# Routed expert tiles of a two-layer network: 28 tiles of one expert and four tiles that hold two experts, in place of 36 tiles of one expert

## The chip, the cores and the metric

One NeuronCore of a Trainium2 chip runs the whole program in one launch. The metric is device time in microseconds (us), from the first to the last instruction of the core, taken as the median of several runs of the compiled kernel. All data are fp32. The engines are named as in the profile: PE (TensorE, its matrix multiplications), PEld (its loads of stationary weights), DVE (VectorE), ACT (ScalarE), POOL (GpSimd), SP (SyncE, which here only issues DMAs).

## The reference

Four stages update `x` of 32 rows with 64 tokens of 128 features: attention, a routed expert layer, an autocorrelation stage, and a gated layer with block-wise 4-bit rounding. The change is in the second:

```python
def _L0_ffn_ref(x, Wr, W1, b1, W2, b2):          # x: (32, 64, 128), 8 experts, F_FF = 512, K = 2
    logits = x.mean(axis=1) @ Wr
    top_scores, top_idx = jax.lax.top_k(logits, K)
    weights = jax.nn.softmax(top_scores, axis=-1)
    W1s, b1s = (W1[top_idx], b1[top_idx])
    W2s, b2s = (W2[top_idx], b2[top_idx])
    h = jnp.einsum('btd,bkdf->bktf', x, W1s) + b1s[:, :, None, :]
    h = jax.nn.gelu(h, approximate=False)
    y = jnp.einsum('bktf,bkfd->bktd', h, W2s) + b2s[:, :, None, :]
    return jnp.einsum('bk,bktd->btd', weights, y)
...
x = x + jnp.tanh(g_ffn[0]) * _L0_ffn_ref(_layernorm(x, axis=-1), ...)
```

Each of the 32 rows picks two of eight experts, by its mean over the tokens. So there are 64 pairs of a row and an expert, and each pair is a two-layer network of 128 to 512 to 128 features on 64 tokens.

## The kernel before, in words

The program is written engine by engine, each engine's instructions in a fixed order with semaphores between them. The expert stage works on tiles of two rows (`RPT = 2`, 128 tokens). A tile has one expert, so an expert with an odd number of rows leaves half a tile empty; the program therefore always runs `MOE_TILES = (32 * 2 + 8) / 2 = 36` tiles of 72 slots. Which rows and which expert a tile has is data, computed on the chip; the number of tiles and the order of the instructions are not.

**The routing chain** runs between the second normalisation and the first tile. DVE takes the logits, finds the two best experts and makes one-hot rows (L899 to L907). PE counts rows per expert and the rank of each row (L1365, L1366), DVE turns counts into numbers of tiles (`tcol`, L911, L912), PE sums them over experts (L1369, L1370), DVE compares the sums with the tile numbers (`tend`, L917) and computes each row's slot (`base2`, `slot_t`, `slot_k`, L918 to L922); PE adds up `tend` (L1374) and DVE writes `experts` (L924), the expert of each tile. From one-hot rows of slots (`ohs`, `ohb`, L926, L928), PE packs four row numbers into one code (L1380) and DVE writes `packed` (L932). PE fills the waits of this chain with parts of the next attention stage, which stand between the routing products in its program: `context_tiles` (L1322) and `context_kv` (L1344, with a bias product at L1330).

**The weights.** All experts' weights are loaded to SBUF early (`wall`, 514 KB per expert). SP copies those of one tile into one of six buffers (`feed`, L325 and L328): it reads the expert's number from `experts`, then, from the seventh copy on, waits until the tile that used the buffer has done its second product (`y2_done`), and issues the DMA. Tile `j` uses buffer `j % 6`:

```python
            def feed(j):
                e = sp.value_load(experts[0:1, j:j + 1], min_val=0, max_val=E - 1)
                if j >= 6:
                    sp.wait_ge(m["y2_done"], j - 5)
                sp.dma_start(wbuf[j % 6], wall[:, bass.ds(e, 1), :] ...).then_inc(w_sem[j % 6], 16)
```

**A tile's path.** POOL copies the two rows' tokens into `xg` (`gather`, L413 and L420; between groups of gathers it also works on the 4-bit weights of the last stage, L424 to L437). PE multiplies (`hidden`, L1403): four products of 128x128 weights with 128 tokens. ACT applies Gelu with the expert's bias (`gelu`, L631). PE multiplies again (`second`, L1414): four products accumulated in one bank. DVE adds the result, times the row's weight, to that row of `acc` (`collect`, L960). An fp32 product shows as two records of PE and two of PEld. PE's order is two tiles ahead:

```python
            hidden(0)
            hidden(1)
            for j in range(MOE_TILES):
                if j + 2 < MOE_TILES:
                    hidden(j + 2)
                second(j)
```

A **block** below is one `hidden` or one `second` of one tile: eight records of PE in a row. Other places that the prediction speaks of: `values` (L1159), products on one half of the array's columns (64 of 128, both halves in turn), with `project` before and after it (L1150, L1151); `weigh_values` (L1252), the same with 18 columns of tokens; and POOL's powers for the normalisation (`powers`, L267 to L271) with the small table `codes` behind them (L406).

Of the kernel before, what the change touches and what calls it, by code (L numbers as in the profile page):

```python
# [35 lines left out]
MOE_TILES = (B * TOPK + E * (RPT - 1)) // RPT  # L36
SLOTS = RPT * MOE_TILES
NCOL = max(B, MOE_TILES)
# [9 lines left out]
CODE_MAX = RADIX ** RPC - 1  # L48
CTX_BANK = (4, 6, 7, 4)
# [9 lines left out]
    ("wo0", 2 * D), ("bv_col", 32), ("wo_t", D), ("wr", E), ("iota_e", E), ("iota_s", SLOTS), ("iota_j", MOE_TILES), ("before_b", B), ("ones", P),  # L59
# [43 lines left out]
def build(nc, a):  # L103
    with ExitStack() as ctx:
# [60 lines left out]
        wbuf = [carve(10240 + WEXP * i, WEXP) for i in range(4)] + [carve(25472 + WEXP * i, WEXP) for i in range(2)]  # L165
# [37 lines left out]
        tcol, tend, base2, rank = sm(NCOL), sm(MOE_TILES), sm(E), sm(E)  # L203
        slot_t, slot_k, ohs, ohb, ohw = sm(2, E), sm(2), sm(2, SLOTS), sm(SLOTS), sm(SLOTS)
        codes, packed, experts = sm(RPC), sm(CODES).bitcast(I32), sm(MOE_TILES).bitcast(I32)
# [19 lines left out]
        floors_set hsc_ready xsc_ready rolled_made codes_set xn_d xv_done xm_done xd_done xq_done xqt_done xqt_used gate_done gu_done sg_done hh_done hv_done hm_done hd_done hq_done hq_last ht_done ht_used dn_done x4_done out_done dve_d""".split()  # L225
# [79 lines left out]
        def _(sp):  # L305
# [17 lines left out]
            def feed(j):  # L323

                e = sp.value_load(experts[0:1, j:j + 1], min_val=0, max_val=E - 1)  # L325
# [4 lines left out]
            for j in range(MOE_TILES):  # L330
                feed(j)
# [12 lines left out]
        def _(pool):  # L344
# [6 lines left out]
            pool.memset(acc[:, B:ROWS, :], 0.0).then_inc(m["spare_zero"], 1)  # L351
# [49 lines left out]
            powers(pool, 8, 12)  # L401
            powers(pool, 12, 15)
            powers(pool, 15, 16)
            pool.wait_ge(m["ld_rest"], 16)
            for k in range(RPC):
                pool.tensor_scalar(codes[0:B, k:k + 1], pc("bcol", B), -float(k % RPT), float(RADIX ** k), ALU.add, ALU.mult).then_inc(m["codes_set"], 1)  # L406
# [4 lines left out]
            def gather(first, last):  # L411
                for i in range(first, last):
                    code = pool.value_load(packed[0:1, i:i + 1], min_val=0, max_val=CODE_MAX)  # L413
                    rows = [((code // RADIX ** k) % RADIX).with_bounds(min_val=0, max_val=ROWS - 1) for k in range(RPC)]
# [95 lines left out]
        def _(act):  # L510
# [115 lines left out]
            def gelu(j):  # L626

                act.wait_ge(m["h_done"], j + 1)

                for c in range(FC):  # L630
                    ins = act.activation(hg[j % 3][:, c, :], ps[:, j % 3, RPT * S * c:RPT * S * (c + 1)], ACT.Gelu,  # L631
                                         bias=wbuf[j % 6][:, FF + FC * D + c:FF + FC * D + c + 1])
                ins.then_inc(m["hg_done"], 1)
# [157 lines left out]
        def _(dve):  # L791
# [119 lines left out]
            sr.step(dve.tensor_scalar(tcol[0:E], ps[0:E, 1, 0:NCOL], 1.0 / RPT, (RPT - 1) / (2.0 * RPT), ALU.mult, ALU.add))  # L911
            dve.tensor_scalar(tcol[0:E], tcol[0:E], 1.5 * 2 ** 23, 1.5 * 2 ** 23, ALU.add, ALU.subtract).then_inc(m["route_in"], 1)  # L912
# [4 lines left out]
            dve.tensor_tensor(tend[0:E], ps[0:E, 2, P:P + MOE_TILES], pc("iota_j", E), ALU.is_le).then_inc(m["route_in"], 1)  # L917
            sr.step(dve.scalar_tensor_tensor(base2[0:B], ps[0:B, 0, 0:E], float(RPT), rank[0:B], ALU.mult, ALU.add))  # L918
# [6 lines left out]
            for k in range(2):  # L925
                sr.did(dve.tensor_scalar(ohs[0:B, k, :], pc("iota_s", B), slot_k[0:B, k:k + 1], None, ALU.is_equal))  # L926
# [874 lines left out]
```

## Time and profile before

| | |
|---|---|
| median of 3 runs | 275.0 us (274.87 to 275.17) |
| span of the profiled execution | 274.8 us |
| its busy PE / PEld / DVE / ACT / POOL | 253.9 / 196.4 / 190.7 / 164.6 / 131.0 us |
| expert stage, first to last of its products | 106.9 to 172.5 us of the span |
| mean granted TensorE clock over the span | 0.988 |

The profiled execution has no other time than its span; the runs of the table lie 0.1 to 0.4 us above it. Times in the rows further on are us from the start of the span unless they are marked ns. In groups of instructions, the numbers behind the bar are busy time and the mean ns of one; then the idle time of the engine just before them, with what ended it. The chain is the work that ended last, followed back from the end. The duration of a PE record includes its way through the array, so records overlap and blocks are timed by the distance of their starts.

### The profile page before, as it was taken

The numbers are of one execution on the slowest core, as the hardware profiler recorded it, in microseconds if no ns is written. First come the engines' busy times: TensorE is split into PE (matmuls) and PEld (weight loads), VectorE is DVE, ScalarE is ACT, GpSimd is POOL, SyncE is SP. The second block draws the span as 40 slices with busy tenths as digits, with TensorE's granted clock in tenths as the row PEclk, the third lists the DMA queues.
The fourth block names the chain that finished last, engine by engine and source line by source line (L and its number), as shares of the span: only waits on it lengthen the run. The fifth ranks groups of instructions, "written<-read, shape, count | busy, mean of one in ns | idle before, by whom it ended". The sixth has DMA issues, their size and how long they took to land.

```text
span 274.8 us, 6251 instructions
## 1 busy us (share of the span) xinstructions
PE 253.9 (92%) x2152; PEld 196.4 (71%) x2152; DVE 190.7 (69%) x494; ACT 164.6 (60%) x384; POOL 131.0 (48%) x207
## 2 busy tenths in 40 slices
PE   8999999999899989999999999979998784989886
PEld 6655376666577868999999999665785442766675
DVE  3898688888988763253222223885769989999993
ACT  2369985666488654675566667473445793354453
POOL 4566579999402403218992220275066633353230
PEclk9999999999999998999999999999999999799999
DMA  6999000000000209776777771000000000000111
GB/s 191 379 348 403 13 4 2 2 4 0 2 2 4 76 20 377 300 289 265 296 300 291 292 290 63 2 1 1 4 0 0 0 0 2 0 19 23 38 39 38
DMA packets 12191, 30.11 MB, mean 110 GB/s; under 512 B 1024, under 2 KB 5248, under 8 KB 12032
## 3 DMA queue, kind: packets, MB, share of 16 engines
q1 hardware_dynamic: 12160, 29.71, 28.5%
q8 instruction: 17, 0.28, 0.4%
q14 instruction: 14, 0.11, 0.1%
HBM read 9.71 MB, written 1.05 MB: 39 GB/s over the span
## 4 chain that ended last, share of the span: by engine, by line
PE 64%; DVE 20%; issue 7%; ACT 5%; POOL 2%; DVEq 0%; POOLq 0%
PE ps L1403 12%; PE ps L1414 12%; PE ps L1252 6%; DVE s_region L294 4%; PE ps L1226 4%; PE ps L1239 4%; PE ps L1159 3%; DVE s_region L1090 3%; PE ps L1542 3%; PE ps L1150 2%; DVE s_small L1095 2%; PE ps L1262 2%; PE ps L1151 2%; PE ps L1344 2%; DVE s_small L237 2%
## 5 line engine op out<-in xcount | busy, mean ns | idle before, releaser
L631 ACT ACTIVATE s_region<-ps,s_region 128x128 f32<-128x128 f32 x144 | 40.8, 371 | 21.8 <-PE ps L1403 21.8
L960 DVE SCALAR_TENSOR_TENSOR s_ctxT<-ps,s_region,s_ctxT 128x64 f32 x72 | 18.1, 281 | 43.8 <-PE ps L1414 43.8
L1403 PE MATMUL ps<-s_region 128*128 128x128 f32 x288 | 38.0, 276 | 0.3 <-issue 0.3
L1414 PE MATMUL ps<-s_region 128*128 128x128 f32 x288 | 37.9, 275 | 0.0
L1403 PEld LDWEIGHTS ps<-s_region 128*128 128x128 f32 x288 | 34.9, 192 | 0.7 <-issue 0.7
L1414 PEld LDWEIGHTS ps<-s_region 128*128 128x128 f32 x288 | 35.0, 192 | 0.2 <-issue 0.2
L420 POOL COPY s_region<-s_xt 128x64 f32 x72 | 14.8, 234 | 32.3 <-PE ps L1403 24.5
L574 ACT COPY s_region<-ps 128x512 f32<-128x512 f32 x32 | 17.2, 592 | 16.2 <-PE ps L1239 16.2
L830 DVE TENSOR_REDUCE s_small<-ps 128x16 f32<-128x1024 f32 x16 | 19.6, 1224 | 9.7 <-PE ps L1226 9.7
L1599 PE MATMUL ps<-s_region 128*128 128x352 f32 x64 | 21.1, 469 | 5.3 <-DVE s_region L1090 3.7
L301 POOL TENSOR_TENSOR s_region<-s_region,s_small 128x704 f32<-128x704 f32 (+2 forms) x11 | 14.6, 1330 | 22.0 <-DVE s_region L294 21.7
L364 POOL TENSOR_SCALAR s_region<-s_region 128x512 f32<-128x512 f32 x16 | 24.7, 1569 | 0.0
L267 POOL TENSOR_SCALAR s_small<-s_small 128x4 f32<-128x4 f32 (+3 forms) x14 | 3.2, 232 | 40.8 <-DVE s_small L244 40.8
L294 DVE SCALAR_TENSOR_TENSOR s_region<-s_region 128x704 f32<-128x704 f32 (+2 forms) x28 | 20.4, 728 | 0.5
L1599 PEld LDWEIGHTS ps<-s_region 128*128 128x128 f32 x64 | 11.3, 189 | 11.9 <-DVE s_region L1090 5.2
L838 DVE TENSOR_TENSOR s_region<-ps,s_small 128x1024 f32<-128x1024 f32 x16 | 18.7, 1170 | 0.1
L1252 PE MATMUL ps<-s_region 128*64 128x18 f32 x512 | 17.8, 212 | 0.8 <-ACT s_region L574 0.7
L1252 PEld LDWEIGHTS ps<-s_region 128*64 128x64 f32 x512 | 16.3, 138 | 3.0 <-ACT s_region L574 1.4
L569 ACT ACTIVATE s_region<-s_region 128x1024 f32<-128x1024 f32 x16 | 17.2, 1073 | 1.1 <-DVE s_region L838 1.1
L1226 PE MATMUL ps<-s_region 64*64 64x512 f32 x128 | 17.4, 615 | 0.0
L1239 PE MATMUL ps<-s_par,s_region 128*128 128x128 f32 x128 | 16.7, 273 | 0.0
L269 POOL TENSOR_TENSOR s_small<-s_small,s_par 128x4 f32<-128x4 f32 (+3 forms) x14 | 16.7, 1191 | 0.0
(230 smaller groups left out, 528.7 us busy)
## 6 DMA issues: line engine op xcount, KB each, us to landing
s_region<-s_wall SPq DMA_DIRECT2D x36, 514.0 KB, 3.0
s_wall<-wall SPq DMA_DIRECT2D x8, 514.0 KB, 9.3
s_par<-par SPq DMA_DIRECT2D x1, 1280.0 KB, 10.5
s_x<-x SPq DMA_DIRECT2D x2, 512.0 KB, 6.8
out<-s_x SPq DMA_DIRECT2D x6, 128.0 KB, 1.8
s_region<-ffn SPq DMA_DIRECT2D x1, 560.0 KB, 3.6
s_ctxT<-ctxT SPq DMA_DIRECT2D x2, 256.0 KB, 4.0
s_ctxT<-ctxT SPq DMA_DIRECT2D x1, 512.0 KB, 6.7
```

Source lines behind the costliest of these rows:

```text
L294: return eng.scalar_tensor_tensor(out, mag, 1.5, z, ALU.max, ALU.subtract)
L364: pool.tensor_scalar(kbd[g % 2][:, j, :], cols, hmask[:, j:j + 1], None, ALU.mult).then_inc(m["kbd_done"], 1)
L631: ins = act.activation(hg[j % 3][:, c, :], ps[:, j % 3, RPT * S * c:RPT * S * (c + 1)], ACT.Gelu, bias=wbuf[j % 6][:, FF + FC * D + c:FF + ...
L830: dve.tensor_reduce(mx[t % 2], scores(t % 2), AX, ALU.max).then_inc(m["mx_done"], 1)
L838: dve.tensor_tensor(ssub[t % 2], scores(t % 2), mx[t % 2].unsqueeze(2).broadcast_to([P, H, S]), ALU.subtract).then_inc(m["s_sub"], 1)
L960: dve.scalar_tensor_tensor(row, ps[:, 4 + j % 2, S * k:S * k + S], w, row, ALU.mult, ALU.add).then_inc(m["acc_done"], 1)
L1226: ins = mm(ps[S * row:S * row + S, 2 * (t % 2) + half, :], qT[rows, 2 * t + row, :], kbd[g % 2][rows, :, k:k + S], start=True, stop=True)
L1239: ins = tr(ps[:, 4 + half, P * k:P * k + P], pr[t % 2][:, c:c + P], ident)
L1252: ins = mm(ps[S * row:S * row + S, 6 + t % 2, n * c:n * c + n], pT[t % 2][:, c, S * row:S * row + S], vbd[:, 2 * t + row, c, :], start=Tru ...
L1403: ins = mm(ps[:, j % 3, RPT * S * c:RPT * S * (c + 1)], w[:, P * c:P * c + P], xg[j % 4], start=True, stop=True)
L1414: ins = mm(ps[:, 4 + j % 2, 0:RPT * S], w[:, FF + D * c:FF + D * c + D], hg[j % 3][:, c, :], start=(c == 0), stop=(c == FC - 1))
L1599: ins = mm(ps[:, 1 + 2 * n + t, 0:MLP], xqT[(q // 2) % 2][:, lo:lo + P], wguT[:, MT * P * n:MT * P * n + MLP], start=True, stop=True)
```

## The change

The slots become exactly 64, in 32 tiles. The rows of an expert are paired into whole tiles of one expert; the odd row of an expert goes to a mixed tile, with the odd row of another expert. The program has 28 plain tiles and four mixed ones (tiles 6, 13, 20 and 27; after that four plain ones). If the experts have fewer odd rows, mixed tiles hold two rows of one expert, and the program is the same.

A mixed tile needs two copies of weights, so the copies are numbered apart from the tiles: `FEEDS = 28 + 8 = 36` copies through the same six buffers (`RING`). Copy `f` waits for the tile that read the buffer before, `tile_of(f - 6)`. In a mixed tile each product is made in four parts of 64 weight columns by 64 tokens, one row's tokens with one expert's weights on one half of the array's columns at a time: `pieces` puts both rows on the two halves, and a second turn swaps them. ACT does Gelu in eight parts of 64 tokens, since the bias differs.

The routing chain computes pairs (`qcol`) and odd rows (`ocol`) for each expert, and places of pairs and odd rows. POOL prepares its tables (`routing_tables`: ten instructions, and the four of `codes`, which move with it ahead of two calls of `powers`). The zeroed spare rows of `acc` are no longer needed.

```diff
-MOE_TILES = (B * TOPK + E * (RPT - 1)) // RPT
-SLOTS = RPT * MOE_TILES
+SLOTS = B * TOPK
+MOE_TILES = SLOTS // RPT
+MIXED = E // RPT
+PLAIN = MOE_TILES - MIXED
+RUN = PLAIN // MIXED - 1
+FEEDS = PLAIN + E
+RING = 6
...
+def mixed(j):
+    return j < MIXED * (RUN + 1) and j % (RUN + 1) == RUN
+def first_feed(j):
+    return j + min(j // (RUN + 1), MIXED)
+def tile_of(f):
+    group = RUN + RPT
+    return f - MIXED if f >= MIXED * group else (RUN + 1) * (f // group) + min(f % group, RUN)
...
-                if j >= 6:
-                    sp.wait_ge(m["y2_done"], j - 5)
-                sp.dma_start(wbuf[j % 6], wall[:, bass.ds(e, 1), :].rearrange("p a w -> p (a w)")).then_inc(w_sem[j % 6], 16)
+                if f >= RING:
+                    sp.wait_ge(m["y2_done"], tile_of(f - RING) + 1)
+                sp.dma_start(wbuf[f % RING], wall[:, bass.ds(e, 1), :].rearrange("p a w -> p (a w)")).then_inc(w_sem[f % RING], 16)
...
+            routing_tables()
             powers(pool, 12, 15)
             powers(pool, 15, 16)
...
+                parts, f = (RPT if mixed(j) else 1), first_feed(j)
+                n = RPT * S // parts
+                for k in range(parts):
+                    for c in range(FC):
+                        b1 = wbuf[(f + k) % RING][:, FF + FC * D + c:FF + FC * D + c + 1]
+                        ins = act.activation(hg[j % 3][:, c, n * k:n * k + n], ps[:, j % 3, ...], ACT.Gelu, bias=b1)
...
+            def pieces(j, turn, lo):
+                for half in range(2):
+                    k = half ^ turn
+                    stay = wbuf[(first_feed(j) + k) % RING][:, lo + S * half:lo + S * half + S]
+                    yield slice(S * half, S * half + S), slice(S * k, S * k + S), stay
             def hidden(j):
-                pe.wait_ge(w_sem[j % 6], 16 * (j // 6 + 1))
+                for k in range(RPT if mixed(j) else 1):
+                    pe.wait_ge(w_sem[(f + k) % RING], 16 * ((f + k) // RING + 1))
...
                 for c in range(FC):
+                    if mixed(j):
+                        for turn in range(RPT):
+                            for parts, cols, stay in pieces(j, turn, P * c):
+                                ins = mm(ps[parts, j % 3, RPT * S * c + cols.start:RPT * S * c + cols.stop], stay, xg[j % 4][:, cols], start=True, stop=True)
```

`second` is changed in the same way. What the routing and the expert stage become on the engines is best seen in the order of instructions.

On PE, around tile 6 (`hidden` of tile 5, `second` of 3, `hidden` of 6, `second` of 4, `hidden` of 7). Names behind "waits" are semaphores: `w0` to `w5` count landed weights of a buffer, `xg_done` gathered rows, `hg_done` Gelus, `acc_done` collected rows. Before:

```order
L1403 MATMUL ps<-s_region 128x128 [waits hg_done,xg_done,w5]
L1403 MATMUL ps<-s_region 128x128 x3
L1414 MATMUL ps<-s_region 128x128 [waits acc_done,hg_done]
L1414 MATMUL ps<-s_region 128x128 x3
L1403 MATMUL ps<-s_region 128x128 [waits hg_done,xg_done,w0]
L1403 MATMUL ps<-s_region 128x128 x3
L1414 MATMUL ps<-s_region 128x128 [waits acc_done,hg_done]
L1414 MATMUL ps<-s_region 128x128 x3
L1403 MATMUL ps<-s_region 128x128 [waits hg_done,xg_done,w1]
```

And now, at the same place:

```order
L1470 MATMUL ps<-s_region 128x128 [waits hg_done,xg_done,w5]
L1470 MATMUL ps<-s_region 128x128 x3
L1487 MATMUL ps<-s_region 128x128 [waits acc_done,hg_done]
L1487 MATMUL ps<-s_region 128x128 x3
L1468 MATMUL ps<-s_region 64x64 [waits xg_done,hg_done,w1,w0]
L1468 MATMUL ps<-s_region 64x64 x15
L1487 MATMUL ps<-s_region 128x128 [waits acc_done,hg_done]
L1487 MATMUL ps<-s_region 128x128 x3
L1470 MATMUL ps<-s_region 128x128 [waits hg_done,xg_done,w2]
```

Tile 6 waits for two buffers and has 16 products of 64x64 where four of 128x128 stood, and tile 7 takes the buffer that tile 8 had.

On DVE, in the routing chain, from the counts per expert to the experts of the tiles (`dve_r` is DVE's own count, a wait for its instruction before). Before:

```order
L912 TENSOR_SCALAR s_small<-s_small 8x36 [waits dve_r]
L914 TENSOR_SCALAR s_small<-s_small 32x1 [waits le_ready]
L915 RECIPROCAL s_small<-s_small 32x1 [waits dve_r]
L917 TENSOR_TENSOR s_small<-ps,s_par 8x36 [waits route_mm,dve_r]
L918 SCALAR_TENSOR_TENSOR s_small<-ps,s_small 32x8
L920 TENSOR_TENSOR s_small<-s_small 32x8 [waits dve_r]
L920 TENSOR_TENSOR s_small<-s_small 32x8
L922 TENSOR_REDUCE s_small<-s_small 32x2 [waits dve_r]
L924 TENSOR_SCALAR s_small<-ps 1x36 [waits route_mm,dve_r]
```

And now:

```order
L958 SCALAR_TENSOR_TENSOR s_small<-s_small 8x36 [waits dve_r]
L960 TENSOR_SCALAR s_small<-s_small 32x1 [waits le_ready]
L961 RECIPROCAL s_small<-s_small 32x1 [waits dve_r]
L964 TENSOR_TENSOR s_small<-ps,s_small 8x72 [waits route_mm,dve_r]
L965 TENSOR_TENSOR s_small<-s_small,ps 32x8
L966 TENSOR_TENSOR s_small<-s_small,ps 32x8
L967 TENSOR_TENSOR s_small<-s_small,ps 32x8 [waits dve_r]
L968 TENSOR_TENSOR s_small<-s_small 32x8 [waits dve_r]
L970 TENSOR_TENSOR s_small<-s_small 32x8 [waits dve_r]
L970 TENSOR_TENSOR s_small<-s_small 32x8
L972 TENSOR_REDUCE s_small<-s_small 32x2 [waits dve_r]
L974 TENSOR_SCALAR s_small<-ps 1x36 [waits route_mm,dve_r]
```

One instruction is new ahead of the part shown (L911 and L912 became L956 to L958), and three are new in place of L918, two of them with a wait for the one before.

On PE, the routing products in the same stretch. Before:

```order
L1369 MATMUL ps<-s_small,s_par 8x36 [waits route_in]
L1370 MATMUL ps<-s_par,s_small 32x8
L1322 MATMUL ps<-s_par,s_ctxN 128x128 [waits cf_used,ld_ctxn]
L1374 MATMUL ps<-s_small,s_par 1x36 [waits tr2_used,route_in]
L1322 MATMUL ps<-s_par,s_ctxN 128x128 [waits ld_ctxn]
```

And now:

```order
L1418 MATMUL ps<-s_small,s_par 8x36 [waits tables_set,route_in]
L1419 MATMUL ps<-s_small,s_par 8x36
L1420 MATMUL ps<-s_small,s_par 8x36
L1421 MATMUL ps<-s_small 32x24
L1422 MATMUL ps<-s_par,s_small 32x8
L1370 MATMUL ps<-s_par,s_ctxN 128x128 [waits cf_used,ld_ctxn]
L1426 MATMUL ps<-s_small 1x36 [waits tr2_used,route_in]
L1427 MATMUL ps<-s_small,s_par 1x36
L1370 MATMUL ps<-s_par,s_ctxN 128x128 [waits ld_ctxn]
```

Two products became five, and one became two.

## Rows read from the trace of the kernel before

**Rows 1.** Chain that ended last, expert stage: start us, us, what.
```profile
106.97 2.88 PE ps L1403 x24
...
127.09 1.13 PE ps L1403 x8
...
134.54 1.13 PE ps L1403 x8
135.67 0.89 PE ps L1414 x8
136.56 0.89 PE ps L1403 x8
```
**Rows 2.** Costliest groups of the page: expert stage's ACT, DVE and POOL lines.
```profile
L631 ACT ACTIVATE s_region<-ps,s_region 128x128 f32<-128x128 f32 x144 | 40.8, 371 | 21.8 <-PE ps L1403 21.8
L960 DVE SCALAR_TENSOR_TENSOR s_ctxT<-ps,s_region,s_ctxT 128x64 f32 x72 | 18.1, 281 | 43.8 <-PE ps L1414 43.8
...
L420 POOL COPY s_region<-s_xt 128x64 f32 x72 | 14.8, 234 | 32.3 <-PE ps L1403 24.5
```
**Rows 3.** Chain, earlier stages: half-array blocks and the whole-array products around them.
```profile
7.57 1.90 PE ps L1159 x32
9.47 1.05 PE ps L1150 x2
...
15.20 0.86 PE ps L1150 x2
...
38.97 1.04 PE ps L1252 x32
```
**Rows 4.** Instructions of line L328 (SP's copies of weights): issue to landing.
```profile
DMA to landing us min/median/max: 2.9/3.0/4.9
```
**Rows 5.** DMA view, issues in 101.6:109.3, then one each from 119.7, 134.4, 149.0, 161.6.
```profile
s_region<-s_wall SPq DMA_DIRECT2D x6, 514.0 KB, 2.9
...
s_region<-s_wall SPq DMA_DIRECT2D x1, 514.0 KB, 4.1
...
s_region<-s_wall SPq DMA_DIRECT2D x1, 514.0 KB, 4.9
...
s_region<-s_wall SPq DMA_DIRECT2D x1, 514.0 KB, 4.0
...
s_region<-s_wall SPq DMA_DIRECT2D x1, 514.0 KB, 4.4
```
**Rows 6.** DMA view, queues in 106.9:172.5: packets, MB, share of 16 engines.
```profile
q8 instruction: 4, 0.07, 0.4%
q14 instruction: 5, 0.04, 0.2%
```
**Rows 7.** Page, DMA queues of the whole span: packets, MB, share of 16 engines.
```profile
q8 instruction: 17, 0.28, 0.4%
```
**Rows 8.** Timeline of SP: six first copies, first waited copy; chain: the block ahead.
```profile
101.69 7.56 SPq L328 DMA_DIRECT2D s_region<-s_wall  x6
...
110.86 0.49 SPq L328 DMA_DIRECT2D s_region<-s_wall  x1
...
109.84 0.89 PE ps L1414 x8
```
**Rows 9.** Timeline, 98.85:100.4, routing: start us, us, engine line op out<-in.
```profile
98.96 0.17 DVE L911 TENSOR_SCALAR s_small<-ps 8x36 f32<-8x36 f32 x1
99.17 0.17 DVE L912 TENSOR_SCALAR s_small<-s_small 8x36 f32<-8x36 f32 x1
...
99.39 0.23 PE L1369 MATMUL ps<-s_small,s_par 8*8 8x36 f32 x2
99.46 0.20 PE L1370 MATMUL ps<-s_par,s_small 8*32 8x8 f32 x2
...
99.88 0.14 DVE L918 SCALAR_TENSOR_TENSOR s_small<-ps,s_small 32x8 f32<-32x8 f32 x1
100.06 0.23 DVE L920 TENSOR_TENSOR s_small<-s_small 32x8 f32<-32x8 f32 x2
```
**Rows 10.** Windows: us, PE PEld DVE ACT POOL busy (x), PEclk, DMA share, GB/s.
```profile
98.00:101.00 3.00, 2.33 (x20) 1.55 (x18) 2.31 (x17) 2.60 (x5) 0.00 (x0) 1.00 0.00 0
102.00:105.00 3.00, 3.00 (x8) 1.87 (x8) 0.77 (x5) 1.17 (x2) 1.14 (x6) 0.50 0.72 285
```
**Rows 11.** Timeline of POOL, 88:96: the wait before `powers` and the table `codes`.
```profile
92.88 0.24 POOL L267 TENSOR_SCALAR s_small<-s_small 128x3 f32<-128x3 f32 x1 [3.74 <-DVE s_small L244]
...
95.22 0.85 POOL L406 TENSOR_SCALAR s_small<-s_par 32x1 f32<-32x1 f32 x4
```

More of the change, by code:

```diff
@@ L163, in build @@
         ctxF = carve(8192, TILES * P)
-        wbuf = [carve(10240 + WEXP * i, WEXP) for i in range(4)] + [carve(25472 + WEXP * i, WEXP) for i in range(2)]
+        wbuf = [carve(10240 + WEXP * i, WEXP) for i in range(RING - 2)] + [carve(25472 + WEXP * i, WEXP) for i in range(2)]
         hg = [carve(14352 + RPT * S * FC * i, FC, RPT * S) for i in range(3)]
@@ L202, in build @@
         oh, mem, wt, wtT = sm(2, E), sm(E), sm(E), sm(B)
-        tcol, tend, base2, rank = sm(NCOL), sm(MOE_TILES), sm(E), sm(E)
+        ncol, qcol, ocol, tend, rank = sm(NCOL), sm(NCOL), sm(NCOL), sm(2, FEEDS), sm(E)
+        pairs_at, odd, odd_at, base2 = sm(E), sm(E), sm(E), sm(E)
+        spans, thresholds, places, fold = sm(3, E), sm(FEEDS), sm(SLOTS), sm(1)
         slot_t, slot_k, ohs, ohb, ohw = sm(2, E), sm(2), sm(2, SLOTS), sm(SLOTS), sm(SLOTS)
-        codes, packed, experts = sm(RPC), sm(CODES).bitcast(I32), sm(MOE_TILES).bitcast(I32)
+        codes, packed, experts = sm(RPC), sm(CODES).bitcast(I32), sm(FEEDS).bitcast(I32)
         v8, s4 = sm(2, 8), sm(2)
@@ L413, in gather @@
                     code = pool.value_load(packed[0:1, i:i + 1], min_val=0, max_val=CODE_MAX)
-                    rows = [((code // RADIX ** k) % RADIX).with_bounds(min_val=0, max_val=ROWS - 1) for k in range(RPC)]
+                    rows = [((code // RADIX ** k) % RADIX).with_bounds(min_val=0, max_val=B - 1) for k in range(RPC)]
                     for j in (2 * i, 2 * i + 1):
@@ L930, in _ @@
             dve.wait_ge(m["route_mm"], 5)
-            empty = float(sum(RADIX ** k * (NONE + k % RPT) for k in range(RPC)))
-            dve.tensor_scalar(packed[0:1], ps[0:1, 0, 0:CODES], empty, None, ALU.add).then_inc(m["packed_ready"], 1)
+            dve.tensor_scalar(packed[0:1], ps[0:1, 0, 0:CODES], float(CODE_MAX), None, ALU.min).then_inc(m["packed_ready"], 1)
             sr.did(dve.tensor_scalar(wt[0:B], oh[0:B, 0, :], lw[0:B, 0:1], None, ALU.mult))
@@ L949, in rows_of @@
                 code = dve.value_load(packed[0:1, i:i + 1], min_val=0, max_val=CODE_MAX)
-                return [((code // RADIX ** k) % RADIX).with_bounds(min_val=0, max_val=ROWS - 1) for k in range(RPC)]
+                return [((code // RADIX ** k) % RADIX).with_bounds(min_val=0, max_val=B - 1) for k in range(RPC)]
             def collect(j, rows):
@@ L1373, in _ @@
             pe.wait_ge(m["tr2_used"], G4)
-            mm(ps[0:1, 3, 0:MOE_TILES], pc("ones", E)[:, 0:1], tend[0:E], start=True, stop=True).then_inc(m["route_mm"], 1)
+            mm(ps[0:1, 3, 0:FEEDS], fold[0:E], tend[0:E, 0], start=True, stop=False)
+            mm(ps[0:1, 3, 0:FEEDS], pc("ones", E)[:, 0:1], tend[0:E, 1], start=False, stop=True).then_inc(m["route_mm"], 1)
             context_tiles(13, 15)
@@ L1412, in second @@
                     pe.wait_ge(m["cf_used"], G4)
-                for c in range(FC):
-                    ins = mm(ps[:, 4 + j % 2, 0:RPT * S], w[:, FF + D * c:FF + D * c + D], hg[j % 3][:, c, :],
-                             start=(c == 0), stop=(c == FC - 1))
+                if mixed(j):
+                    for turn in range(RPT):
+                        for c in range(FC):
+                            for parts, cols, stay in pieces(j, turn, FF + D * c):
+                                ins = mm(ps[parts, 4 + j % 2, cols], stay, hg[j % 3][:, c, cols], start=(c == 0), stop=(c == FC - 1))
+                else:
+                    for c in range(FC):
+                        ins = mm(ps[:, 4 + j % 2, 0:RPT * S], w[:, FF + D * c:FF + D * c + D], hg[j % 3][:, c, :],
+                                 start=(c == 0), stop=(c == FC - 1))
                 ins.then_inc(m["y2_done"], 1)
```

76 lines of the change are left out of this document (50 added, 26 removed).

## The prediction, made before the kernel was run

> **What bounds the kernel now.** I read the chain that ended last first: the expert stage is 65 us of blocks of PE, one behind the other, 0.89 us each [rows 1]. What is to be seen there is that almost nothing stands between them: two blocks take 1.13 us, at 127.1 and 134.5 us, and the rest does not wait. Then the costliest groups: ACT, DVE and POOL sit idle in this stage until PE is done (21.8, 43.8 and 24.5 us) [rows 2]. So PE's blocks are the bound, and a removed block gives back its whole time as long as nothing else comes late. What could is looked up in three more places: the copies of weights, issue to landing [rows 4, 5]; the stretch of routing, whose length moves the whole stage [rows 9, 10]; and two earlier stages where PE already works on halves of the array [rows 3].
>
> **Removed tiles.** Four tiles are eight blocks of 0.89 us [rows 1]: **-7.1 us**. Nothing depends on how the rows fall on the experts: 28 plain and four mixed tiles always run.
>
> **Mixed blocks.** The eight blocks of the four mixed tiles have 16 products of 64 columns of weights by 64 tokens, 32 records, in pairs on the two halves. The trace has no such block, but two close ones. `weigh_values` has the same 32 records of 64 weight columns with 18 columns of tokens: 1.04 us [rows 3]. `values` has 32 with 128 tokens (two calls): 1.90 us [rows 3]. A column costs 0.84 ns (0.86 us over two records of 512 columns [rows 3]), so streams alone explain 16 x 128 x 2 x 0.84 ns / 2 = 1.72 of the 1.90 us: the halves run side by side, and the weight loads are hidden. At 64 tokens streams would take 0.86 us and the load-limited block 1.04 us, so loads set the pace; 46 more columns at the end add 0.04 us. Leaving the half-array form costs 0.19 us (the product after `values` takes 1.05 us, the same without a change of form 0.86 [rows 3]). Sum 1.27 us, 0.38 more than a plain block; eight of them: **+3.0 us**. The bounds are 0 (streams alone, 0.86 us) and +9.6 us (the 1.90 us row with its 0.19); I am near the first since the 1.04 us row is nearest in form.
>
> What the row of `values` shows speaks against a rule. The Trainium skill (TensorE: Matmul & The Clock Gate, Part 3: Packing small matmuls, The mechanism) says that a weight load overlaps a running product only when the row groups differ, and both halves here use all rows. By it, a block would be loads plus streams, and the time that of the fourth rival below. The trace disagrees: at 128 tokens that would be 1.04 + 1.72 = 2.8 us, and it is 1.90.
>
> **Copies of weights.** This is the term that decides. There are 36 copies before and after, but a mixed tile takes two of the six buffers, so the look-ahead falls from six tiles to five for most. Before, the copy of tile j is issued when `second(j-6)` is done, six blocks or 5.4 us ahead of `hidden(j)`; 0.13 us pass until the issue (the block ends at 110.73, SP issues at 110.86 [rows 8]). So 5.2 us are there, and the 36 landings of 2.9 to 4.9 us [rows 4] all fit. Now copies 7 to 12, 15 to 20, 23 to 28 and from 31 on wait for `second(j-5)`: four blocks, 3.57 us, or 3.95 where one of them is mixed, less 0.13. That leaves 3.4 to 3.8 us, in the mean 3.6. A quiet landing (2.9 [rows 5]) still fits. The late ones do not: 4.1, 4.9, 4.0 and 4.4 us [rows 5] exceed 3.6 by 0.5, 1.3, 0.4 and 0.8, 3.0 us in all. What makes them late are loads of code that share the DMA engines: each of these four windows lies at one of the four loads on queue q8 in the stage [rows 6]. I take q8 to be PE's code: 17 loads in the span [rows 7] for 4304 products and weight loads is one per 253 records, and the stage has 72 x 16 = 1152, 4.5 times that. The new stage has 56 x 16 + 8 x 64 = 1408 records, 5.6 times, so five such loads: 3.75 us. In front of a block that waited, the first weight load is bare, as long as the stream of 128 columns, 0.11 us: 0.5 us for five. Then SP: it issues copies 1.41 us apart when nothing holds it ((7.56 - 0.49) / 5 [rows 8]). Two copies are released together by a mixed tile, and SP falls behind by 3 x 1.41 - 3.57 = 0.66 us at the second copy of tiles 13, 20 and 27. That copy has 3.44 - 0.66 = 2.8 us for a landing of 2.9; 0.15 us each, 0.45 in all. The queue q14 (five loads [rows 6]) adds perhaps 0.1. Sum **+4.8 us**, with bounds of 0 (all land in 2.9 to 3.4) and 8 (each code load costs what the 4.9 us landing would, 1.4, and SP's lag 0.3 each).
>
> **Routing chain.** One more waited DVE step before the sums (L911 to L912, 0.21 us); six more PE records at 0.035 us (99.39 to 99.46 for two), 0.21; twice the elements in `tend`, 0.04 (28 more elements cost 0.03 between L918 and L911); three DVE instructions more for `base2`, two of them waited at 0.18 (99.88 to 100.06) and one at 0.08 (two at L920 in 0.23) [rows 9]: 0.9 us in all until `experts` and `packed`. PE's fill-in work behind it has no gap up to the first tile, so the shift arrives. But from 102 to 105 us this work runs at a granted clock of 0.50, the lower of the two levels, after a stretch in which PE was idle part of the time [rows 10]. If that low stretch keeps its place, 0.9 us less of the work lies in it and half of that is saved. Between 0.45 and 0.9 I take **+0.7 us**.
>
> **Costed at nothing, or little.** POOL's gathers and its work on the 4-bit weights hold PE twice for 0.24 us (1.13 less 0.89 [rows 1]). The second hold, before `hidden(16)`, is covered by tile 13's slower blocks: **-0.2 us**; if it isn't, that is lost. Gelu in eight parts takes at most twice its 1.1 us (40.8 / 36 [rows 2]) and has 2.7 us until its `second`; ACT idles 0.6 us per tile (21.8 / 36 [rows 2]). POOL's 14 table instructions at 0.21 us (0.85 / 4) take 3.0 us and lie in its idle 3.74 us before `powers` [rows 11]; if they overran, the last normalisation would move by the difference, 0.3 us at most. DVE has eight rows fewer to add, under PE. The memset that is dropped stood at the start, beside loads.
>
> **Sum.** -7.1 + 3.0 + 4.8 + 0.7 - 0.2 = +1.2 us, against the profiled 274.8: 276.0. The runs lie 0.1 to 0.4 us above that span; with 0.2, **276.2 us**.
>
> **Rivals.**
> 1. *The weights come in time after all* (faster). Place: PE's wait at the first product of `hidden`. Price: the 4.8 us fall away, 271.2 + 0.2 = 271.4 us; with half of them, 273.8. It decides at a landing of 3.4 us in the changed kernel: below it no copy is waited for. For it: the median landing is 3.0 [rows 4], and a code load between two copies may cost less than one beside a copy. Against it: four landings in the old order already took 4.0 to 4.9 [rows 5].
> 2. *The terms cancel*: code loads meet the copies with six blocks, or cost 0.3 us less each: 275 us.
> 3. *The low clock stays longer.* PE waits more in the longer chain and the low stretch lasts into the first tiles; another stretch of 3 us at half speed costs 1.5 us: 277.7 us. Against it: PE was back at 1.00 by 106 us with the fill-in work alone.
> 4. *Loads do not overlap on half-arrays.* A mixed block would take 1.04 + 0.86 + 0.23 = 2.1 us, +9.9 us for eight in place of 3.0; the weights then have more time, some 3 us of their 4.8 fall away: 280 us. The row of 1.90 us speaks against it. It is what the rule of the Trainium skill quoted above (TensorE: Matmul & The Clock Gate) would do here.
>
> **How the numbers follow.** Chances: the forecast 0.58 (275 to 278 us by its bounds on copies and clock), rival 1 0.22, rival 2 0.11, rival 3 0.06, rival 4 0.03. A difference of 0.2% (0.55 us) is about what a measurement of this kernel can tell from none. Faster by more: rival 1 and a small part of the forecast, 0.25. Within: rival 2 and the low end of the forecast, 0.16. Slower: 0.59. The forecast's own range is 275.0 to 278.0; to leave out no more than 2 in 10 the range takes in most of rival 1 and rival 3: 272.0 to 278.2.
>
> **What would show it.** Right: PE's blocks of plain tiles stay at 0.89 us, mixed ones near 1.27; PE idles 4 to 5 us in the stage before first products of `hidden`, released by the DMA, in five or six places; landings of 4 us and more beside q8 loads; the first tile starts at about 107.6 us. Wrong: no such waits (rival 1); mixed blocks over 1.6 us (rival 4); a granted clock of 0.50 beyond 106 us (rival 3).

## The result: slower, and by more than forecast

| | median | runs |
|---|---|---|
| before, beside the changed kernel | 274.96 us | 4: 274.87 to 275.17 |
| changed | 281.76 us | 4: 277.73, 280.43, 283.09, 283.31 |
| before, all later runs beside the experiments | 276.89 us | 64: 274.57 to 281.99 |
| changed, all runs | 281.47 us | 10: 277.73 to 283.31 |

The ratio of the first pair is 1.014, 95% interval 1.008 to 1.020, without the two longest runs of the changed kernel. The medians of all runs stand 4.6 us (1.7%) apart. The forecast was 276.2 us, range 272.0 to 278.2.

First the clock. Span and mean granted clock, before and then changed:

```profile
core 0: 274.8 us, clock 0.988
```
```profile
core 0: 281.5 us, clock 0.964
```

281.5 us is the span of the run of 283.31 us: 1.8 us lie outside it. The windows show where the clock was low in the changed kernel (columns as in [rows 10]):

```profile
98.60:101.00 2.40, 2.04 (x24) 1.58 (x25) 1.53 (x13) 2.00 (x4) 0.00 (x0) 1.00 0.00 0
...
104.40:109.00 4.60, 4.60 (x16) 3.61 (x14) 0.40 (x2) 0.98 (x2) 1.30 (x7) 0.50 0.95 385
109.00:114.60 5.60, 5.60 (x27) 5.54 (x27) 2.29 (x1) 2.48 (x10) 0.86 (x4) 0.50 0.50 204
114.60:120.00 5.40, 5.40 (x50) 5.40 (x50) 1.54 (x6) 3.41 (x12) 1.31 (x6) 1.00 0.48 195
```

The low stretch runs from 101.0 to 114.6 us, through the fill-in work and into the first tiles; before it lasted from 102.0 to 105.4 [rows 10]. Low is 1.2 GHz, the lower of the two levels, 0.50 in the rows. In the last stage, too, the clock is low for 6.8 us in place of 3.4 (from 223.9 and 240.9 us, 3.4 us each). Now the chain that ended last, the lines that answer to [rows 1]:

```profile
109.13 5.42 PE ps L1470 x24
...
121.03 4.14 DMA s_region<-s_wall
125.22 1.16 PE ps L1470 x8
126.38 1.10 PE ps L1484 x32
...
130.26 4.87 DMA s_region<-s_wall
135.12 1.36 issue
136.49 1.15 PE ps L1468 x32
137.64 1.09 PE ps L1487 x8
138.73 0.89 PE ps L1470 x8
```

The first three blocks take 5.42 us where they took 2.88. A plain block is 0.89 us as before. A mixed one (L1468 or L1484, 32 records) takes 1.08 to 1.10, and the plain block behind it 1.09: together 1.28 for the mixed one, 0.39 over a plain one. Two of five waits for weights are seen: the copy is in the chain, and the block that it releases takes 1.16 in place of 0.89, or, a mixed one, 1.15 in place of 1.08. The instructions of the copies (L350, answering to [rows 4]), and the queues between 109.1 and 177.4 us, answering to [rows 6]:

```profile
  PEld ps L1470: 2.7, 4
  PE ps L1470: 1.9, 4
  PEld ps L1468: 1.6, 1
  PE ps L1468: 1.4, 1
...
DMA to landing us min/median/max: 2.9/3.5/4.9
```
```profile
q8 instruction: 5, 0.08, 0.4%
q14 instruction: 5, 0.04, 0.2%
```

PE's idle time at the five places is 1.9 + 1.4 = 3.3 us. The five loads of q8 begin at 122.0, 131.9, 143.7, 156.2 and 166.1 us, the five waits end at 125.2, 136.5, 146.9, 159.4 and 169.3: each some 3 to 5 us behind a load. The longest wait, 1.4 us before the mixed tile 13 (135.12 to 136.49 in the chain), ends with the second copy of that tile: SP issued it 1.47 us behind the first, at 131.73 us, and it landed 1.28 us behind it, at 136.40.

The two traces cut at the same three places (first product of the experts, last product of `second`) add up to the 6.7 us:

| us | before | changed | difference | of it low clock |
|---|---|---|---|---|
| start to first tile | 106.90 | 109.06 | +2.2 | 1.3 |
| stage of the experts | 65.64 | 68.30 | +2.7 | 2.8 |
| behind it | 102.29 | 104.14 | +1.9 | 1.9 |

In the stage 5.58 us lie at half clock: 2.8 us, if such work takes half as long at the full one. Ahead of it, 0.86 us of the 2.2 are the chain (below). The last line is put down to the clock since the tail took 102.3 to 102.5 us in all eight profiles below whose clock did not fall at the first products of the last stage (L1672 here, 46 us behind the stage of the experts). So by this estimate the change itself made about +0.7 us, and the clock 6.0.

### The profile page after: what moved, and what is told of

It reads as the page before. It is cut to its first block, busy times and chain, and to the rows that moved or that the text cites. A ratio compares the mean times of both kernels' runs of the same rounds, so it can differ in the third digit from the quotient of the medians.

```text
span 281.5 us, 6484 instructions
## 1 busy us (share of the span) xinstructions
PE 256.4 (91%) x2288; PEld 195.6 (69%) x2288; DVE 189.2 (67%) x490; ACT 162.8 (58%) x384; POOL 130.8 (46%) x208
## 4 chain that ended last, share of the span: by engine, by line
PE 54%; DVE 20%; DMA 9%; issue 8%; ACT 5%; POOL 2%; SPq 1%; DVEq 0%; POOLq 0%
DMA s_region<-s_wall 8%; PE ps L1470 7%; PE ps L1300 6%; PE ps L1487 6%; DVE s_region L316 4%; PE ps L1274 4%; PE ps L1287 4%; PE ps L1207 3%; DVE s_region L1138 3%; PE ps L1615 2%; DVE s_small L1143 2%; PE ps L1198 2%; PE ps L1392 2%; PE ps L1310 2%; PE ps L1199 2%
## 5 line engine op out<-in xcount | busy, mean ns | idle before, releaser
L676 ACT ACTIVATE s_region<-ps,s_region 128x128 f32<-128x128 f32 (+1 forms) x144 | 39.0, 361 | 26.6 <-PE ps L1470 21.7
L1008 DVE SCALAR_TENSOR_TENSOR s_ctxT<-ps,s_region,s_ctxT 128x64 f32 x64 | 16.1, 281 | 48.5 <-PE ps L1487 42.1
L1470 PE MATMUL ps<-s_region 128*128 128x128 f32 x224 | 32.9, 296 | 1.9 <-DMA s_region<-s_wall 1.9
L1470 PEld LDWEIGHTS ps<-s_region 128*128 128x128 f32 x224 | 29.5, 206 | 3.2 <-DMA s_region<-s_wall 2.7
L461 POOL COPY s_region<-s_xt 128x64 f32 x64 | 13.3, 237 | 37.7 <-PE ps L1470 25.0
L1487 PE MATMUL ps<-s_region 128*128 128x128 f32 x224 | 30.0, 278 | 0.0
L1672 PE MATMUL ps<-s_region 128*128 128x352 f32 x64 | 23.5, 512 | 5.1 <-DVE s_region L1138 3.7
L1487 PEld LDWEIGHTS ps<-s_region 128*128 128x128 f32 x224 | 27.4, 193 | 0.4 <-issue 0.2
L1672 PEld LDWEIGHTS ps<-s_region 128*128 128x128 f32 x64 | 12.3, 205 | 12.7 <-DVE s_region L1138 5.2
```

The costliest lines, as they stand in the source:

```text
L676: ins = act.activation(hg[j % 3][:, c, n * k:n * k + n], ps[:, j % 3, RPT * S * c + n * k:RPT * S * c + n * k + n], ACT.Gelu, bias=b1)
L1470: ins = mm(ps[:, j % 3, RPT * S * c:RPT * S * (c + 1)], w[:, P * c:P * c + P], xg[j % 4], start=True, stop=True)
L1487: ins = mm(ps[:, 4 + j % 2, 0:RPT * S], w[:, FF + D * c:FF + D * c + D], hg[j % 3][:, c, :], start=(c == 0), stop=(c == FC - 1))
L1672: ins = mm(ps[:, 1 + 2 * n + t, 0:MLP], xqT[(q // 2) % 2][:, lo:lo + P], wguT[:, MT * P * n:MT * P * n + MLP], start=True, stop=True)
```

## The experiments

The kernels ran on several chips, each beside runs of the kernel before on the same chip. What each profile shows, read from its trace (us; "first tile" counts from the product that counts the rows per expert, L1413 and its like, at 98.59 us in the changed kernel; "tail" is what follows the stage; "waits filled" means products of PE added in the waits of the routing chain):

| kernel | low at the routing | first tile | stage | tail | span |
|---|---|---|---|---|---|
| before | 102.0, for 3.4 | +8.3 | 65.6 | 102.3 | 274.8 |
| before again (b0) | 100.5, for 10.2 | +9.6 | 67.2 | 102.3 | 277.0 |
| before, chain longer (e4) | 101.2, for 13.7 | +10.5 | 68.2 | 102.3 | 279.2 |
| before, 5 buffers (e2) | none | +6.64 | 69.4 | 103.9 | 278.1 |
| before, waits filled (e6) | none | +6.66 | 66.1 | 102.3 | 273.8 |
| changed | 101.0, for 13.7 | +10.5 | 68.3 | 104.1 | 281.5 |
| changed again (e0) | 102.5, for 10.2 | +10.5 | 66.6 | 104.1 | 280.1 |
| changed, 7 buffers (e1) | 100.0, for 13.7 | +10.5 | 63.2 | 102.4 | 274.5 |
| changed, last wait filled (e7) | 100.6, for 3.4 | +8.7 | 65.4 | 102.5 | 274.5 |
| changed, first two filled (e8) | none | +7.50 | 65.5 | 104.1 | 275.5 |
| changed, all filled (e3) | none | +7.50 | 64.8 | 102.4 | 273.0 |
| changed, 7 buffers, filled (e5) | none | +7.51 | 62.0 | 102.5 | 270.1 |
| the same, plain blocks (e9) | none | +7.50 | 59.3 | 104.2 | 269.9 |

And the granted clock of the runs, as the share of them in which it was low for about 10 us or more, added up over the whole span (mean clock 0.982 or less): before 25 of 64, changed 9 of 10, e1 9 of 10, e2 1 of 4, e4 3 of 4, e3 1 of 10, e5 0 of 6, e6 0 of 12, e7 3 of 12, e8 1 of 12, e9 0 of 2. Where in the span it was low is known of the profiled runs alone.

**A seventh buffer.**

```diff
-RING = 6
+RING = 7
-        wbuf = [carve(10240 + WEXP * i, WEXP) for i in range(RING - 2)] + ...
+        wbuf = [carve(10240 + WEXP * i, WEXP) for i in range(4)] + [carve(16912, WEXP)] + ...
-        wB = carve(17424, SLOTS)
+        wB = carve(15888, SLOTS)
```

> The changed kernel with a seventh buffer for weights, so that every copy is released at least six tiles ahead again. Theory (look-ahead): the waits of PE before the products of `hidden` (3.3 us of idle time in five places, and 0.26 us more in each of the five blocks behind them, 4.6 us in all) vanish, and the span is 4.6 us below that of the changed kernel at the same number of low stretches of the clock: about 277 us with a low stretch of 13.7 us at the routing, about 271.5 us where the clock is low for 3.4 us only. Rival (the DMA engines are the limit: copies that land late hold PE whenever they were issued): at least 3 of the 4.6 us stay, 280 and 275 us. The low stretch of the clock at the routing and the 1.8 us between span and run are not touched by this edit in either theory.

Median 276.89 us (10 runs) against 276.83 (19 runs of before on the same chip), span 274.5 with the long low stretch. The copies' instructions:

```profile
who waited for it (us, times):
busy tenths in 40 slices 0000000000000000000000000000000000000000
DMA to landing us min/median/max: 2.9/3.5/4.6
```

Nobody waited for a copy, though the copies landed as late as in the changed kernel (median 3.5 us in both). So it is the look-ahead that turned late landings into waits: the theory holds, the rival falls. The stage takes 63.2 us with 4.8 us of it at half clock, so 60.8 at full clock by estimate, 4.7 less than the 65.5 of the changed kernel reckoned in the same way.

**Five buffers in the kernel before.**

```diff
-        wbuf = [carve(10240 + WEXP * i, WEXP) for i in range(4)] + [carve(25472 + WEXP * i, WEXP) for i in range(2)]
+        wbuf = [carve(10240 + WEXP * i, WEXP) for i in range(4)] + [carve(25472, WEXP)]
-                if j >= 6:
-                    sp.wait_ge(m["y2_done"], j - 5)
+                if j >= 5:
+                    sp.wait_ge(m["y2_done"], j - 4)
```

> The kernel before with five buffers of weights in place of six, 36 tiles of one expert as before. Theory (look-ahead): copies are released four blocks ahead, 3.57 us less 0.13, for all tiles from the sixth on; so landings over 3.4 us hold PE, as in the changed kernel: 10 of the 30 landings after the sixth were longer than 3.4 us in the kernel before, by 5 us in all at most, and each wait makes the next copies' windows longer; 3 to 6 us slower, 278 to 281 us. Rival (the waits in the changed kernel come from its mixed tiles and its code loads, not from the look-ahead): within 1 us of the kernel before, 275 to 276 us. The low stretches of the clock stay as before (one of 3.4 us at the routing, one in the last stage).

Median 280.20 us (4 runs) against 276.83 (19 runs). The stage takes 69.4 us, 3.7 more than with six, without any low clock in it. The chain has the same pattern as in the changed kernel, without one mixed tile:

```profile
118.08 4.13 DMA s_region<-s_wall
122.20 0.04 issue
122.25 1.16 PE ps L1403 x8
123.41 0.89 PE ps L1414 x8
```

A buffer less for plain tiles costs what was expected (3 to 6 us).

**All waits of the routing filled.** `again(n)` computes a tile of the context's transform a second time, to the same place.

```diff
             context_tiles(9, 11)
+            for n in (9, 10):
+                again(n)
             pe.wait_ge(m["route_in"], 1)
...
             context_tiles(11, 12)
+            pe.wait_ge(m["cf_used"], 1)
+            for n in (12, 12):
+                again(n)
             pe.wait_ge(m["route_in"], 2)
...
             context_tiles(13, 15)
+            for n in (12, 13, 14):
+                again(n)
             pe.wait_ge(m["route_in"], 4)
```

> The changed kernel, with seven products of PE more in the three waits of the routing chain: tiles of the context's transform that are computed a second time to the same place, 0.22 us each, 0.44 us, 0.44 us and 0.66 us in idle gaps of 0.6, 0.5 and 0.7 us. Theory (idle time of PE in the routing stretch lowers the clock): the low stretch at the routing vanishes or shrinks to 3.4 us, the first tile of the experts starts at 107 to 108 us, and the run is 4 to 6 us faster than the changed kernel, 276 to 278 us with the 1.8 us outside the span. Rival (the low stretch does not depend on that idle time): the low stretch of 13.7 us stays, and the time is that of the changed kernel or up to 0.3 us more, 281 to 283 us.

Median 275.63 us (10 runs, 274.11 to 280.73). The windows:

```profile
98.20:101.20 3.00, 3.00 (x34) 2.57 (x34) 2.04 (x16) 2.45 (x5) 0.00 (x0) 1.00 0.02 5
101.20:104.40 3.20, 3.03 (x25) 2.23 (x24) 1.56 (x10) 1.17 (x2) 0.72 (x4) 1.00 0.29 120
```

PE is busy 3.00 of 3.00 us ahead of the place where it had been 2.04 of 2.40, and the clock stays at 1.00. Work that computes nothing new made the changed kernel 5.8 us faster in the median, with its waits for weights still there. On the same chip e1, whose routing waits are those of the changed kernel, had 10 us and more of low clock in 9 of 10 runs, and this kernel in one of 10. The theory holds.

**A longer chain alone, in the kernel before.**

```diff
             sr.step(dve.tensor_scalar(tcol[0:E], ps[0:E, 1, 0:NCOL], ...))
+            for _ in range(4):
+                sr.step(dve.tensor_scalar(tcol[0:E], tcol[0:E], 1.0, None, ALU.mult))
```

> The kernel before with its routing chain made 0.8 us longer: four more DVE steps that multiply a column of eight rows by 1.0, each waited for. Theory (the longer chain, in which PE waits more, makes the low stretch at the routing last longer): the low stretch grows from 3.4 to 10 us or more, and the time by the 0.8 us and 3 to 5 us more: 279 to 281 us. Rival (the low stretch in the changed kernel comes from its other parts: the additional small products, the tables, or what the engines do after the routing): the low stretch stays at 3.4 us, and the time rises by 0.8 us at most, 275.4 to 275.8 us. The time between span and run stays at 0.1 to 0.4 us in both.

Four runs: 275.46, 280.37, 280.47, 281.06. The one at 275.46 is near before's best plus 0.8, as the rival has it; the other three are near the theory's range. The time lay 1.8 to 1.9 us above the span, not 0.1 to 0.4. In the profile of 281.06:

```profile
98.30:101.10 2.80, 1.84 (x17) 1.42 (x18) 2.02 (x15) 2.38 (x5) 0.00 (x0) 1.00 0.00 0
101.25:114.80 13.55, 13.13 (x57) 11.24 (x56) 4.18 (x12) 4.58 (x14) 2.90 (x14) 0.50 0.60 234
```

The low stretch of the changed kernel, 13.7 us, appears in a kernel that has nothing of the change but 0.8 us more in the chain; so the change's other parts are not needed for it. But the kernel before has 10 us and more of low clock in 25 of 64 runs without any edit, so three of four runs do not show that the longer chain made it more frequent.

**The changed kernel again.**

> The changed kernel once more, unaltered, with more runs of it and of the kernel before on one chip. Theory (the change by itself is worth little, and most of the measured difference was the length of the clock's low stretches, which both kernels have and which differ from run to run): the runs of both kernels are spread over 275 to 283 us, the median of the changed one lies 0 to 3 us above that of before, and its lowest within 1 us of before's lowest (274.6). Rival (the longer routing chain makes the low stretch at the routing long in nearly every run of the changed kernel): its median stays at 281 us or more, 4 to 6 us above that of before, with hardly a run under 278 us.

Median 281.46 us (6 runs, 280.51 to 282.65) against 276.51 (17 runs of before, 275.02 to 281.83). The rival wins: 10 us and more of low clock are there in all six runs of the changed kernel, and in 5 of the 17 of the kernel before.

**Both edits.** The seventh buffer and the seven products together.

> The changed kernel with both edits: the seventh buffer for weights, and the seven products of PE in the three waits of the routing chain. Theory (the two losses are separate: waits for weights by the look-ahead, low clock by idle time of PE at the routing): the stage of the experts takes 61 us (65.6 in the kernel before), no wait over 0.2 us in it; the clock is not low at the routing in most runs; span 269 to 270 us with one or two low stretches in the last stage, median run 271 to 272 us, 1.5 to 2% faster than before. Rival (without the waits PE would not have been slowed by the low clock, or the copies hold it up otherwise): the two gains overlap, the median is not more than 1 us below that of the run with the PE products alone (275.6).

Median 272.50 us (6 runs, 271.75 to 273.46) against 276.51: ratio 0.985, interval 0.980 to 0.991, and 9.0 us below the changed kernel on the same chip. The clock and the stage:

```profile
core 0: 270.1 us, clock 0.994
```
```profile
98.06:105.57 7.51, 7.34 (x64) 5.97 (x63) 3.96 (x27) 3.81 (x8) 1.31 (x7) 1.00 0.31 125
105.57:167.60 62.03, 61.50 (x706) 59.32 (x706) 19.95 (x67) 41.57 (x148) 27.26 (x67) 1.00 0.74 293
```

The losses are separate and nearly add: 4.6 us (e1) and 5.8 (e3) apart, 9.0 together. The stage is 1 us longer than expected, and 0.5 us of waits are left (0.21, 0.12 and 0.20, before tiles 2, 8 and 13). Here it is SP's pace, a copy every 1.4 us, that holds PE and not the ring alone: the copy for tile 8 was issued at 114.86 us, 1.4 us after its buffer came free.

**The filled waits in the kernel before.** Two, one and two products in the same places.

> The kernel before with five additional products of PE in the waits of its routing chain (two, one and two tiles of the context's transform computed a second time). Theory (idle time of PE in the routing stretch lowers the clock there, in both kernels): no low stretch at the routing in most runs, median 274 to 275 us where the kernel before has 276.8 on the same chip, and few runs above 277. Rival (the low stretches at the routing came and went by chance in the first look, and the additional products do nothing): the median is that of before within 0.5 us, and runs of 278 to 281 us appear as often.

Median 275.49 us (12 runs, 274.66 to 277.37) against 276.51; none of the runs has 10 us or more of low clock, 5 of the 17 of before on the same chip have. So the kernel before seems to lose to the same cause, only less often: 1.0 us of its median, though the ratio's interval, 0.993 to 1.000, reaches to no change.

**Which wait.** Only the last wait filled (e7), only the first two (e8).

> The changed kernel with additional products of PE only in the last of the three waits of the routing chain (three products, 0.66 us), the first two waits idle as in the changed kernel. Theory (the low stretch grows long where a wait of PE still lies inside it: in five profiles it lasted 10.2 to 13.7 us where the last wait came after its start, and 3.4 us or nothing otherwise): with the last wait filled the clock may still fall, but comes back after 3.4 us; median 276 to 278 us, few runs over 280. Rival (the fall is set by the idle time of the whole stretch, and once fallen it stays long): the low stretch is 10 us and more in most runs, as in the changed kernel, median 280 to 282 us.

> The changed kernel with additional products of PE only in the first two of the three waits of the routing chain (two each, 0.44 us), the last wait of 0.6 to 0.8 us idle. Theory (the last wait decides): where the clock falls it stays low for 10 us and more; it falls less often than in the changed kernel since less time is idle ahead of it; median between 277 and 282 us, with some runs over 280. Rival (the idle time of the whole stretch decides): four products of seven keep the clock up in most runs, median 276 to 277 us, as with all seven.

Medians 277.11 us (12 runs, two over 280) and 276.58 (12 runs, one over 280), against 277.52 (23 runs of before on the same chip). In e7 the clock fell and came back:

```profile
98.00:100.50 2.50, 2.15 (x26) 1.70 (x27) 1.65 (x13) 2.11 (x4) 0.00 (x0) 1.00 0.02 7
100.60:103.90 3.30, 3.30 (x20) 2.49 (x19) 1.81 (x11) 0.77 (x2) 0.00 (x0) 0.50 0.22 90
104.00:107.00 3.00, 3.00 (x20) 2.51 (x19) 0.65 (x3) 1.17 (x2) 1.70 (x8) 1.00 0.98 395
```

Over the profiles with a low stretch here: the product behind the last wait (L1433 and its like) starts inside it in five (changed, e0, e1, e4, b0), and these lasted 10.2 to 13.7 us; in the kernel before the product started 0.6 us ahead of it, and in e7 no wait was open: 3.4 us in both. That fits the theory of e7. But e8, which leaves the last wait idle, did as well, as its rival has it. So filling either part helps; which of them decides is not settled.

**Mixed tiles as plain ones**, with both edits of e5.

```diff
-                    if mixed(j):
+                    if False:
```

> The changed kernel with the seventh buffer and the seven products of PE, and its four mixed tiles computed as plain ones: both rows of a mixed tile go through the weights of its first expert, so the second expert's part of these tiles is left out; copies, gathers, gelu and sums are as they were. It prices the mixed blocks alone. Theory (0.41 us for each of eight blocks, as the rows of the changed kernel show): the stage of the experts takes 3.3 us less than with mixed blocks, 58.7 us, and the span is 3.3 us below at the same low stretches. Rival (waits for weights or for ACT take the place of the blocks' time): 1.5 us or less.

Median 271.20 us (2 runs). The stage takes 59.3 us, 2.7 less than in e5; its waits are 0.6 us longer (one of 0.85 us). So eight mixed blocks cost 3.3 us, the theory's value, and the rival falls. The span does not show it: it is 0.1 us below that of e5, since the clock was low twice in the last stage here and the tail is 1.7 us longer.

**The kernel before, span and time of one run.**

> The kernel before, unaltered, to have the span and the time of one and the same execution. Theory: the time lies 1.8 us above the span, as in every other run whose span is known; the profiled execution of before (274.8 us of span, low stretches at the routing and in the last stage) then stands for a run of 276.6 us, and the runs of 274.9 to 275.2 us for spans of 273.1 to 273.4 with a low stretch less. Rival: for this kernel the time lies 0.1 to 0.4 us above the span, as the prediction took it, and the changed kernel adds 1.5 us outside of its span.

Span 277.0 us, time 278.85. In 138 of the 146 runs of all kernels whose span is known the time lies 1.76 to 1.88 us above it; the eight others, at 1.96 to 2.93, are runs of e3 and e5. The rival falls, and with it a step of the prediction (below). This profile also has a long low stretch in the kernel before:

```profile
97.90:100.50 2.60, 2.15 (x18) 1.53 (x18) 1.92 (x14) 2.18 (x4) 0.00 (x0) 1.00 0.03 6
100.55:110.70 10.15, 10.05 (x42) 8.35 (x43) 3.71 (x10) 2.98 (x8) 2.14 (x10) 0.50 0.79 311
110.80:114.00 3.20, 3.20 (x31) 3.20 (x30) 0.54 (x2) 2.35 (x9) 0.86 (x4) 1.00 0.00 0
```

## Why the prediction was wrong

The direction was right, the terms of the sum mostly too; the time was outside the range by two steps, neither of them about the tiles.

**The step that failed: the third rival.** "The low clock stays longer" had a chance of 0.06 and a price of 1.5 us. It came in 9 of 10 runs of the changed kernel (two by their profiles, seven by their mean clock), and the low stretch was 10.2 and 13.7 us long at the routing in the two profiles. In the first of them it cost 4.1 us more than before at the routing and in the first tiles (1.3 + 2.8), and 1.9 more in the last stage, in place of 1.5 us. Its sign, a granted clock of 0.50 beyond 106 us, stands in the windows above. Against it the prediction put one row, "PE was back at 1.00 by 106 us with the fill-in work alone". That row was one execution: in 25 of the 64 later runs of the same kernel the clock was low for about 10 us or more in the span, and in b0 for 10.2 us at the routing. The routing term even counted the low clock as a saving ("half of that is saved"). The mechanism that the rival named, more waiting of PE in the chain, is the one that the runs show: seven products in the waits take the long stretch away (e3, and again e5 on the chip of e0), and e4 fits from the other side with four runs. Which of the three waits decides is not settled (e7, e8).

The price as the runs have it: before's spans lie at 272.8 to 273.5 us in most runs of clock 0.994, 276.7 to 277.5 at 0.975, and 279.8 to 280.2 at 0.97. The Trainium skill (TensorE: Matmul & The Clock Gate, Part 1: The HAM clock gate, What's actually happening) says that the number of products at the lower level before the return differs from run to run, and that this ramp costs under 1% of a typical kernel's span. The runs agree with the first: 3.4 and 10.2 us at the same place of the kernel before. They do not bear out the second for a program whose clock falls on its way: from 273 to 280 us it is 2.5%.

**The second step: "The runs lie 0.1 to 0.4 us above that span."** The span of 274.8 us and the runs of 274.9 to 275.2 were taken for the same state. They were not: 274.8 us of span is a run of 276.6, and by the later runs of 275 us (span 273.3, clock 0.994) the ones shown had about 3.4 us less low clock. The sum's 276.0 us of span is a run of 277.8 us. The fastest run of the changed kernel is 277.73 us, span 275.9, clock 0.994; that this meets the sum is partly luck, since the sum started from a profile at 0.988.

**Removed tiles**: right, a plain block is 0.89 us in both. The two holds by POOL, of which the prediction took one off (-0.2), are both gone: no product of the changed kernel's stage waits for POOL.

**Mixed blocks**: forecast 1.27 us and +3.0, measured 1.28 and +3.1 by the rows, +3.3 by e9. The fourth rival, loads that do not overlap, wanted 2.1 us and falls. The Trainium skill (TensorE: Matmul & The Clock Gate, Part 3: Packing small matmuls, The mechanism) says that a weight load overlaps running products only when their row groups differ; the 1.28 us measured on these column halves speak against it.

**Copies of weights**: right in place and number (five waits behind five loads of q8), forecast +4.8. The first rival, weights that come in time, falls with them. In the profiled run 3.3 us of idle time and 1.2 us in the blocks behind it (0.27 in each of four plain ones, 0.07 in the mixed one) make 4.5. By the distance of starts a plain block behind a wait takes 1.00 us (146.89 to 147.89), so its bare load costs the 0.11 us that it was priced at; the other 0.16 is time that the idle time misses, since records overlap. The seventh buffer takes 2.8 us off the stage between e3 and e5, 4.0 between e3 and e1 and 4.7 between the changed kernel and e1, all at full clock: the waits differ from run to run, 2.3 to 3.4 us of idle time, from tile 8 on, in the five profiles of the changed kernel's tiles with six buffers. The second copy of a mixed tile was priced at 0.15 us; that of tile 13 ended a wait of 1.4 us. That the loads of code make the copies late stays a coincidence in time, five for five in the changed kernel's profile; no run took the loads away.

**Routing chain**: forecast 0.9, cut to 0.7 for the low clock. At full clock the first tile comes 7.50 us behind the product that counts the rows (e3, e8), in place of 6.64 (e2): +0.86. The 0.9 was right, and the cut had the wrong sign.

**Sum.** For the stage alone the terms came to +0.5 us (-7.1 + 3.0 + 4.8 - 0.2). Without the clock, chain +0.9 and a stage 0.1 to 0.8 us shorter (65.5, 65.4 and 64.8 in e8, e7 and e3 against 65.6) come to +0.1 to +0.8 us, at the edge of what a measurement of this kernel can tell; against the 66.1 of e6 it would be half a microsecond less. So the terms nearly cancel, as the second rival had it, but the runs do not come out at its 275 us. By the same estimate the rest of the 4.6 us in the median is how long TensorE runs at its lower level.

## What to carry to other kernels

Before a sum is made against a profiled execution, look up its granted clock and what its run's time was; one profile shows one draw of the clock, and a stage near an idle stretch of PE may come out some 5 us apart. A change that lengthens a chain in which PE waits is priced with the clock behind it, and a few products that repeat work in those waits were cheap insurance here: with them and one more buffer this change turned from 1.7% slower to 1.5% faster. When a tile starts to take two buffers of a ring, count the look-ahead in tiles again, against the longest landing and not the median.

## What was not expected of the hardware

TensorE stayed at its lower level for up to 13.7 us, through the last 10.2 of them with work all the time: 4.60 of 4.60 and 5.60 of 5.60 us busy at 0.50 in the windows above. The low stretch at the routing lasted 3.4 us in one profile of the kernel before and 10.2 in another, 13.7 and 10.2 in two profiles of the changed one. In the last stage its place counts too: where a low stretch began 46 us behind the stage of the experts (both profiles of the changed kernel, e2, e8, e9) the tail took 103.9 to 104.2 us, and 102.3 to 102.5 elsewhere, in two cases (e3, e6) with as many microseconds of low clock. What makes a stretch last is not settled.
